# Layer 1 softmax: weighted values and sums of weights from one pass over the weights, the sums moved to their rows by a shuffle on VectorE

## The reference

```python
h = _rmsnorm(x, ln1_w)
qkv = jnp.einsum('bsh,oh->bso', h, wqkv)      # 16 q heads, 4 k and 4 v heads of 8
q, k = _apply_rope(q, cos, sin), _apply_rope(k, cos, sin)
scores = jnp.einsum('bqhd,bkhd->bhqk', q, k) * scale
scores = jnp.where(causal[None, None], scores, jnp.finfo(scores.dtype).min)
probs = jax.nn.softmax(scores, axis=-1)
attn = jnp.einsum('bhqk,bkhd->bqhd', probs, v).reshape(B, S, NH * HD)
x = x + jnp.einsum('bso,ho->bsh', attn, wo)
```

## Time and profile before

| | |
|---|---|
| median of 3 runs | 1948.61 us (1946.26 to 1956.49) |
| profiled execution, its own time | 1937.43 us |
| its span from first to last instruction | 1935.4 us |
| mean granted clock of TensorE | 0.960 |
| busy: PE / DVE / ACT / POOL | 1674.1 / 1238.5 / 1009.3 / 253.9 us |
| L1079, the two products | 3072 instructions, from 56.4 to 832.8 us |
| L1557, L1559, L2049 | 32 each |

### The profile page before, as it was taken

One profiled execution on the slowest core, in us unless ns is written; L12 is line 12 of the kernel. 1 busy time (PEld: TensorE's weight loads), 2 busy tenths in 40 slices (PEclk: granted clock), 3 DMA queues, 4 the chain that ended last, 5 costly groups with the idle time before them and its releaser, 6 DMA issues.

```text
span 1935.4 us, 65540 instructions
## 1 busy us (share of the span) xinstructions
PE 1674.1 (86%) x25348; PEld 1273.5 (66%) x25364; DVE 1238.5 (64%) x3535; ACT 1009.3 (52%) x2322; POOL 253.9 (13%) x271
## 2 busy tenths in 40 slices
PE   5999999979888898958998898897889889988866
PEld 3777776757666776745676676765577666676656
DVE  5677677756556666646676766765666666676535
ACT  3555555544555555524655566553544455544445
POOL 0000110000000000030111011101121112110063
PEclk9999999999999999979999999998999999999978
DMA  4333334431222211331222122210222111221244
GB/s 164 135 145 144 155 152 174 187 122 42 62 68 68 79 45 56 102 104 43 78 68 68 59 81 80 62 36 25 64 68 61 43 52 53 68 63 55 75 143 120
DMA packets 97379, 167.82 MB, mean 87 GB/s; under 512 B 15145, under 2 KB 65593, under 8 KB 93882
## 3 DMA queue, kind: packets, MB, share of 16 engines
q1 hardware_dynamic: 87322, 141.59, 21.8%
q0 software_dynamic: 9888, 23.71, 4.1%
HBM read 86.42 MB, written 78.80 MB: 85 GB/s over the span
## 4 chain that ended last, share of the span: by engine, by line
PE 52%; DVE 17%; issue 11%; ACT 11%; SPq 4%; DMA 2%; DVEq 1%; POOL 1%; POOLq 0%; ACTq 0%
PE psum L1007 5%; PE psum L851 4%; PE psum L885 3%; PE psum L997 3%; PE psum L1309 3%; PE psum L1199 3%; PE psum L1297 2%; PE psum L896 2%; PE psum L1045 2%; PE psum L932 2%; PE psum L1224 2%; PE psum L1093 2%; PE psum L936 2%; PE psum L1128 2%; ACT pts L1553 2%
## 5 line engine op out<-in xcount | busy, mean ns | idle before, releaser
L1553 ACT ACTIVATE pts<-psum 128x512 f32<-128x512 f32 x192 | 99.2, 604 | 162.1 <-PE psum L1045 161.4
L725 POOL DMA_INDIRECT rows<-h,recA x64 | 62.2, 972 | 780.7 <-DVE recA L1795 662.9
L1007 PE MATMUL psum<-wall,xT_s 128*128 128x512 f32 x256 | 130.3, 656 | 0.1
L749 POOL DMA_INDIRECT rows<-xn,recC x32 | 36.6, 1143 | 667.1 <-DVE recC L2249 612.9
L885 PE MATMUL psum<-txT,wall 128*128 128x128 f32 x864 | 117.0, 279 | 1.9 <-issue 1.5
L1158 PE MATMUL psum<-xT_s,wall 128*128 128x256 f32 x512 | 115.7, 379 | 0.0
L885 PEld LDWEIGHTS psum<-txT,wall 128*128 128x128 f32 x864 | 109.4, 197 | 4.5 <-issue 2.0
L896 PE MATMUL psum<-wall,tg 128*128 128x128 f32 (+1 forms) x720 | 109.2, 287 | 2.6 <-DVE tg L1743 1.9
L2058 DVE TENSOR_REDUCE mneg<-psum 128x2 f32<-128x512 f32 x128 | 79.4, 684 | 40.2 <-PE psum L1025 39.2
L1158 PEld LDWEIGHTS psum<-xT_s,wall 128*128 128x128 f32 x512 | 96.1, 190 | 13.2 <-issue 0.8
L896 PEld LDWEIGHTS psum<-wall,tg 128*128 128x128 f32 x720 | 94.8, 199 | 7.5 <-DVE tg L1743 5.2
(11 more groups left out here) (273 smaller groups left out, 4237.5 us busy)
## 6 DMA issues: line engine op xcount, KB each, us to landing
wall<-in_wB SPq DMA_DIRECT2D x84, 384.0 KB, 3.0
outs<-pbd SPq DMA_DIRECT2D x16, 1024.0 KB, 7.5
mixed_rows<-pbd SPq DMA_DIRECT2D x16, 899.5 KB, 9.6
wall<-in_wD SPq DMA_DIRECT2D x24, 578.0 KB, 3.7
tx<-rows SPq DMA_DIRECT2D x132, 64.0 KB, 2.8
rows<-pbd SPq DMA_DIRECT2D x64, 128.0 KB, 1.7
rows<-pbd SPq DMA_DIRECT2D x8, 1024.0 KB, 3.9
outs<-ty SPq DMA_DIRECT2D x108, 64.0 KB, 1.6
```

Source lines behind the costliest of these rows:

```text
L725: nc.gpsimd.indirect_dma_start(rows, bass.IndirectOffsetOnAxis(ap=slotsA[:, c:c + 1], axis=0), h2[:, t, :], None).then_inc(sem("scattered" ...
L1007: mm(bank(f"{name}{t}{c}"), xnT[:, t * P:(t + 1) * P], wqkv0[:, off + c * 512:off + (c + 1) * 512], start=True, stop=True).then_inc(*fills ...
L1553: af(pT[:, n, :], bank(f"e{n}"), ACT.Exp, scale=float(HD) ** -0.5).then_inc(*frees(f"e{n}"))
```

## The change

The sums of the weights are no longer made by matmuls of their own. The 32 columns of `v9` for one key head, of which 8 held values and 24 zeros, now hold 8 columns of values, 8 of zeros (by the parity of the query head) and, 16 columns on, 8 of ones and 8 of zeros in the same manner. Two of four query heads share one half of the bank's columns instead of all four sharing one, so one pass over `pT` gives a 128x256 result in which, of each 32 rows, the first 16 are values and the last 16 the sums that belong to them. `ones32` is gone.

On DVE a new step `sums_moved(t)` shuffles the bank into `rden` so that the sums stand on the rows of their values. ACT takes Ln and Exp of 128x256 there, and DVE's product is 128x256 and has two halves. `sums_moved(0)` stands where `weighted(0)` was, `weighted(0)` moves behind `rows_given`, and `sums_moved(1)` stands ahead of `weighted(1)`. The output projection adds two halves, with `woR` in two parts, so it has 4 matmuls a sequence instead of 2.

```diff
-        woR = wa[:, 5376:5504]
+        woR = wa[:, 5376:5632].rearrange("p (a n) -> p a n", a=2)
...
-        aT = aden[:, 0:N]
-        rden = aden[:, N:2 * N].rearrange("p (t n) -> p t n", t=NT)
+        aT = aden[:, 0:2 * N].rearrange("p (t a n) -> p t a n", t=NT, a=2)
+        rden = aden[:, 2 * N:4 * N].rearrange("p (t n) -> p t n", t=NT)
...
-            g.memset(ones32[:, :, :], 0.0).then_inc(sem("zeros"), 1)
-            g.wait_ge(sem("zeros"), 3)
+            g.wait_ge(sem("zeros"), 2)
             for j in range(GR):
-                r = j ^ 2
-                g.memset(ones32[:, j, r * HD:(r + 1) * HD], 1.0).then_inc(sem("zeros"), 1)
+                first = 2 * HD + j % 2 * HD
+                g.memset(v9[:, :, j, first:first + HD], 1.0).then_inc(sem("zeros"), 1)
...
                 for t in range(NT):
-                    last = mm(bank("wo")[:, t * P:(t + 1) * P], aT[:, t * P:(t + 1) * P], woR, start=True, stop=True)
+                    for a in range(2):
+                        last = mm(bank("wo")[:, t * P:(t + 1) * P], aT[:, t, a, :], woR[:, a, :], start=(a == 0), stop=(a == 1))
...
-                        for i in range(2):
-                            for j in range(GR):
-                                for g in range(NKV):
-                                    n = 4 * part + g
-                                    pe.wait_ge(*read_out(f"e{n}"))
-                                    values = v9[:, NKV * (part // 2) + g, j, :] if i == 0 else ones32[:, j, :]
-                                    last = mm(bank(f"pa{t}")[32 * g:32 * g + 32, i * P:(i + 1) * P], values, pT[:, n, j * P:(j + 1) * P],
-                                              start=(part == parts[0] and i == 0 and j == 0), stop=(part == parts[-1] and i == 1 and j == GR - 1))
+                        for j in range(GR):
+                            for g in range(NKV):
+                                n = 4 * part + g
+                                pe.wait_ge(*read_out(f"e{n}"))
+                                last = mm(bank(f"pa{t}")[32 * g:32 * g + 32, j // 2 * P:(j // 2 + 1) * P], v9[:, NKV * (part // 2) + g, j, :], pT[:, n, j * P:(j + 1) * P],
+                                          start=(part == parts[0] and j == 0), stop=(part == parts[-1] and j == GR - 1))
...
                 def inverse(t):
-                    act.wait_ge(*filled(f"pa{t}"))
-                    af(rden[:, t, :], bank(f"pa{t}")[:, P:2 * P], ACT.Ln).then_inc(*signals("act_chain"))
+                    act.wait_ge(*given("den_ready", t + 1))
+                    af(rden[:, t, :], rden[:, t, :], ACT.Ln).then_inc(*signals("act_chain"))
...
+                def sums_moved(t):
+
+                    dve.wait_ge(*filled(f"pa{t}"))
+                    dve.sem_inc(sem("copy_turn"), 1)
+                    v.stream_shuffle(rden[:, t, :], bank(f"pa{t}")[:, 0:2 * P], [16 + i % 16 for i in range(32)]).then_inc(*signals("den_ready"))
...
                 def weighted(t):
-                    dve.wait_ge(*filled(f"pa{t}"))
                     dve.wait_ge(*given("rden_ready", t + 1))
-                    v.tensor_tensor(aT[:, t * P:(t + 1) * P], bank(f"pa{t}")[:, 0:P], rden[:, t, :], ALU.mult).then_inc(*frees(f"pa{t}"))
+                    v.tensor_tensor(aT[:, t, :, :], bank(f"pa{t}")[:, 0:2 * P].rearrange("p (a n) -> p a n", a=2), rden[:, t, :].rearrange("p (a n) -> p a n", a=2), ALU.mult).then_inc(*frees(f"pa{t}"))
...
-                for first in (2 * HD, 2 * 32):
+                for first in (0, 2 * 32):
...
                 head_scale()
+                sums_moved(0)
+                rows_given()
                 weighted(0)
-                rows_given()
                 head_turned()
                 tile_step(6)
+                sums_moved(1)
                 weighted(1)
```

More of the change, by code:

```diff
@@ L183 @@
           "xnT_ready": 1, "xr_ready": 1, "x_free": 1},
-    "A": {"act_chain": 2, "kr_ready": 1, "kx_ready": 1, "dve_chain": 16, "ek": 4, "eq": 4, "k0_part": 3, "k0_ready": 1, "rden_ready": 2, "q0_part": 3, "q0_ready": 1, "rope_ready": 1, "aT_ready": 1, "o_ready": 2},
+    "A": {"act_chain": 2, "kr_ready": 1, "kx_ready": 1, "dve_chain": 16, "ek": 4, "eq": 4, "k0_part": 3, "k0_ready": 1, "den_ready": 2, "rden_ready": 2, "q0_part": 3, "q0_ready": 1, "rope_ready": 1, "aT_ready": 1, "o_ready": 2},
     "G": {"act_chain": 3, "counted": 1, "dve_chain": 14, "eg_ready": 1, "h2_free": 1, "h2_ready": 1, "lg_ready": 1, "recA_stored": 1, "rms2_rstd": 1, "x2_ready": 1, "scattered": 1, "slots_ready": 1},
@@ L267, in build @@
         v9 = v9s[:, 0:NT * NKV * GR * 32].rearrange("p (a j c) -> p a j c", a=NT * NKV, j=GR)
-        ones32 = sb("ones32", [P, GR, 32])
         pts = sb("pts", [P, 12 * 512])
-        aden = sb("aden", [P, 2 * N])
+        aden = sb("aden", [P, 4 * N])
         xk = x1
@@ L460, in build @@
         blk = ctx.enter_context(nc.Block())
-        NLOAD, NFIRST, ZEROS = [0], [0], 6 + GR
+        NLOAD, NFIRST, ZEROS = [0], [0], 5 + GR
         @blk.sync
@@ L2395 @@
     ang = np.concatenate([ang, ang], -1).T
-    woR = I["L0_ffn_wo"].T
+    woR = np.zeros((P, 2, D), np.float32)
+    for n in range(NHF):
+        g, j = n // GR, (n % GR) ^ 2
+        first = 32 * g + j % 2 * HD
+        woR[first:first + HD, j // 2] = I["L0_ffn_wo"].T[n * HD:(n + 1) * HD]
     ropec = np.zeros((P, 2, N), np.float32)
```

## The result

The kernel after takes 1962.97 us in the median (20 executions, 1957.32 to 1970.02), the kernel before 1950.62 on the same chip: ratio 1.0058, 95% interval 1.0048 to 1.0068. The forecast was 1962.3, in the range 1947 to 1977.

The account below looks back on a forecast made before the run. VectorE's chain at the body's end was taken to bound AHG, SyncE's queue to the load of x AHGBL. Terms 3.9 + 4.2 + 8.5 - 5.9 + 3.3 - 0.3 = +13.7 us on the median 1948.61 gave 1962.3, range 1947 to 1977.

Parts of the forecast that it names:

- AHG (3.9 + 7 x 0.52 + 8.5): AHG bodies: longer VectorE end +3.9 us, doubled output projection 0.52 us a body, clock falls +8.5 us.
- outside: Before the first slots and behind the last: longer load and memsets at the start counted 0; table has +0.5 us.
- the removed PE work returns nothing: Products for the sums, 2.7 us a body, 43 us in all, become idle time in AHG and AHGBL.
- The shuffle, the wider product, the doubled projection: AHG bodies: shuffle 0.34, load 0.08, product 0.34 for 0.20, together +0.56 us; projection +0.52 us.
- The clock in AHG: Idle of 2.7 us at AHG ends halves the clock at five of seven, 1.7 us each, +8.5 us.
- AHGBL: the failed step: AHGBL loop: slots +1.5 us, falls behind h mostly gone -8.9, longer moved falls +1.5; together -5.9 us.
- AGB: AGB body: start +1.5 us and a moved fall of about 2.4 us, end gains 0.5; +3.3 us net.
- R1: Not slower: AHG keeps its clock and AHGBL gets its own back; -1.5 us, 1947; chance 0.15.
- R2: Clock as it was everywhere: +10.3 us, 1959; chance 0.12.
- R3: Longer falls: every AHG end loses 3.1 us, AHGBL loses at both places; +36 us, 1984; chance 0.13.
- R4: Faster, PE is the bound after all: 16 x 1.6 = 26 us return, 1923; chance 0.05.
- R5: Shuffle costs its upper bound or drains DVE: +0.3 us at 7 + 7 places, +4 us, within the forecast's range.

Follow-up runs that it names:

- the pair again: Both kernels, before and after the change, profiled once more without an edit: spans 1947.0 us before and 1962.3 us after.
- before again: The kernel before, unchanged, profiled a second time: one execution, 1949.03 us, span 1947.0 us.
- after again: The kernel after, unchanged, measured and profiled a second time: 1959.25 us, ratio to before 1.0040.
- no shuffle: The kernel after without the two shuffles, ScalarE taking exponentials of the pass's result itself, output not normalised: 1953.58 us, ratio to before 1.0023.
- projection once: The kernel after with the output projection's products made once, half the heads left out of the output: 1959.93 us, ratio to before 1.0045.
- SyncE moved: The kernel after with 24 more semaphore instructions at the head of SyncE's program: 1959.21 us, ratio to before 1.0049.
- shuffle ahead: The kernel after with the first tile's shuffle ahead of head_scale and its product behind head_turned: 1953.16 us, ratio to before 1.0011.
- head early, one pass / two: Next group's head moved to the middle of the body: in the kernel after 1914.12 us, ratio 0.9814; in the kernel before 1938.64 us, 0.9935.
- pass twice: The kernel after with its one pass over the weights made twice into the same sums: 1964.22 us, ratio to before 1.0066.
- before: projection twice: The kernel before with each matmul of the output projection made twice, same result: 1956.6 us, ratio to before 1.0022.
- before: no sums: The kernel before without the matmuls that make the sums, ScalarE using the weights themselves, output not normalised: 1952.75 us, ratio 1.0001.

## Why the prediction was right in its total and wrong in its terms

Terms of the sum against both pairs of profiles, in us:

| | predicted | after less before | the pair again |
|---|---|---|---|
| AHG (3.9 + 7 x 0.52 + 8.5) | +16.0 | +10.2 | +10.4 |
| to AHGBL and in it | -5.9 | +9.8 | +9.8 |
| AGB and behind it (3.3 - 0.3) | +3.0 | +2.9 | -6.4 |
| outside | +0.5 | +8.3 | +1.5 |
| sum | +13.6 | +31.3 | +15.3 |

**That the removed PE work returns nothing: right.** No sums at all gives 1.0001 (0.9986 to 1.0016), where 26 to 43 us would have come back had PE been the bound.

**The shuffle, the wider product, the doubled projection: right in mechanism, a little too dear.** Where no fall is open the AHG period grew from 43.49 to 44.31, by 0.82; predicted were 1.08. Taking the shuffle away gives back 0.33, taking the doubling away 0.30, and by difference 0.19 is left for the wider product, Ln and Exp, which no run took apart. Load and shuffle are 0.45 us as rows, predicted 0.50. (The trace agrees with the Trainium skill, "VectorE: DVE Perf Modes", the perf-mode tier table, that no fast mode is to be hoped for: 0.44 us beside 0.41 for the copy of the same shape.) The round trip of shuffle, Ln and Exp in front of L2099 did stay hidden in AHG.

**The clock in AHG: mechanism right, size too large.** There are falls in AHG, where there had been none, and filling PE again removes them. But I expected five bodies to pay 1.7 us, 8.5 in all. Two paid, 3.0 and 1.6 us: 4.6. The step that failed is that the fall would come behind the second idle stretch of 2.7 us, on the next body's first projections. Five of six came behind the first, of about 1.6 us, and four of these slowed only a pass that had idle time behind it. That rows show no fall below 1.9 us of idle was also a misreading of the trace of before. In its second level half clock follows idle stretches of 1.22 and 1.47 us; the second of them, with the clock of the stretch behind it:

```profile
1592.65 1.22 PE L885 MATMUL psum<-txT,wall 128*128 128x128 f32 x8 [1.47 <-issue]
...
1593.62:1597.03 3.41, 3.41 (x66) 0.50 0.02 5
```

(That activity releases the clock, as the Trainium skill has it in "TensorE: Matmul & The Clock Gate", part 1, agrees with the falls that went when the pass was made twice.)

**AHGBL: the failed step, with the wrong sign, 15.7 us off.** I had the five falls behind h vanish and nothing else change. Timeline of PE in after, one body:

```profile
618.08 0.71 PE L894 MATMUL psum<-wall,tg 128*128 128x128 f32 x4 [2.44 <-DVE tg L1740]
620.45 0.69 PE L849 MATMUL psum<-ident,xr 128*128 128x128 f32 x2 [1.66 <-DVE aden L2051]
621.05 5.97 PE L1090 MATMUL psum<-xT_s,wall 128*128 128x256 f32 x16
...
638.75 0.43 PE L849 MATMUL psum<-ident,h 128*128 128x128 f32 x2 [3.17 <-DVE h L1990]
639.01 5.30 PE L1006 MATMUL psum<-wall,xT_s 128*128 128x512 f32 x8
```

and the granted clock in the stretches behind both idle times:

```profile
618.85:625.68 6.83, 5.23 (x13) 4.05 (x14) 2.08 (x5) 2.76 (x6) 2.41 (x3) 0.50 0.36 115
...
639.33:642.74 3.41, 3.41 (x5) 1.33 (x4) 3.41 (x7) 1.73 (x5) 0.00 (x0) 0.50 0.00 0
```

The idle before h did shrink, to 3.2 us (predicted 2.9), and the fall behind it from 6.8 us to 3.4, but it is there, which the prediction had named as a sign of being wrong, and the new one at the loop's start with it: from the first AHGBL slots to the last, 12 falls and 64.9 us at half clock against 7 and 44.4. What differs from the first profile of before, though, is on SyncE. Chain of waits of after from the record to the load of x, then that of before for the same instructions:

```profile
616.48 0.36 SPq L643
...
618.79 0.32 SPq L528
619.14 0.70 issue
619.90 0.70 issue
620.62 0.71 issue
621.37 0.70 SPq L530
622.07 0.69 issue
...
634.30 2.70 DMA x<-in_x
```

```profile
598.75 0.36 SPq L644
...
601.15 0.27 SPq L529
601.44 0.15 SPq L529
601.85 0.35 SPq L530
602.39 0.35 SPq L531
602.75 0.06 issue
```

At the first tile's load SyncE's instructions come 0.7 us apart in after. From the slots to the issue of the load of x, and from there to the next slots, it is:

| mean of five bodies, us | slots to load of x | load of x to next slots |
|---|---|---|
| before / before again | 16.05 / 17.06 | 44.03 / 43.04 |
| after / after again | 18.17 / 18.17 | 43.95 / 43.92 |
| no shuffle / projection once / SyncE moved | 17.57 / 17.65 / 17.67 | 43.85 / 43.62 / 43.69 |
| shuffle ahead | 17.40 | 43.36 |
| head early, one pass / two | 17.37 / 16.44 | 41.41 / 43.01 |
| pass twice / before: projection twice / before: no sums | 17.72 / 17.32 / 17.63 | 43.20 / 43.10 / 43.84 |

Against the first profile of before, whose chain runs through the load of x as that of after does, the whole 2.0 us a body are SyncE standing in a piece of its program that the change does not touch, and the stretch behind the load is the same (44.03 and 43.95) although the fall behind h is half as long: that gain of 8.9 us in all did not come. Against the second profile the sum can't be split so. There PE does not stand before the transpose of h. It stands 5.4 us at the loop's start, behind the late Ln, and half clock follows there and not behind h; that is the place to which the prediction had moved the falls of after, and the period is the same 60.1 us. What after loses against this typical execution is shown only as a sum, 2.0 us a body; that the load of x goes out 1.1 us later and that falls lie at both places are two parts of it, and no run took them apart. Why SyncE stands is open: it is not the one pass, since the kernel before with its projection doubled is at 17.32 us too, and moving SyncE's code by 24 instructions took off no more (0.5 us) than edits on other engines did. My prediction named this queue as the chain and then put no uncertainty on it.

**AGB: right for the profile shown, wrong for the typical execution.** The first profile of before was of its fastest execution, and as the other runs have it an untypically smooth one. In its second, and in all three two-pass or 128-instruction variants, AGB and the period behind it took 82.8 to 86.5 us; in every kernel with half the instructions in the pass they took 73.7 to 78.5. Here the one-pass kernel gains back 6.4 of the 9.8 us that it loses in AHGBL. That the shorter pass is what shortens this stretch the runs show; that PE's instructions reach it too late is an inference from the 0.7 us pieces, and no run made it separately.

**Rivals.** R1 was priced for an idle length between 1.9 and 2.3 us as the point that decides, and falls came behind 1.59 us; AHGBL did not get its clock back. R2 is refuted by the AHG falls, R3 happened in its second half only (falls at both places in AHGBL), R4 by the runs without sums. R5's upper bound for the shuffle, 0.7 us, was not reached. The total of the forecast was met by luck: measured less predicted, in the second pair, AHG is 5.6 us below, AGB 9.4 below, AHGBL 15.7 above and the rest 1.0 above, and these nearly cancel.

## What to carry to other kernels

Work taken from an engine that is not on the chain comes back only after the chain has been moved onto it: here the same edit cost 7 to 12 us with the next group's head at the end of the body and saved 24.5 us with it in the middle. Before a filler is removed, look at what will be idle around it and what runs first after the idle time: a fall of the clock costs nothing if it lands on work with slack behind it. And profile the kernel before twice when single-digit microseconds matter: the first profile of before, 0.7% under the median, lacked a stall in AGB that its second profile and three variants had (AGB 58.0 to 59.5 us against 52.3).

## What the runs showed of the hardware

- An engine can start its instructions 0.7 us apart although the trace shows nothing that they wait for: PE in the unrolled AGB body behind 112 instructions of a pass (100 in the kernel with the pass made twice), SyncE in the AHGBL loop. The kernel before showed it on PE in one execution (AGB 59.51 us) and not in the other (52.26). The cause is open.
- In five of six AHGBL bodies of the second profile of before ScalarE's Ln started 5.1 us after the end of PE's pass that it waits for, and in the first profile 0.1 us after it, with the same period of 60.1 us: PE's idle time only changed places, from before h (4.94 us) to the loop's start (5.4 us).
- The pattern load of the shuffle (LOAD_MASK_SELECT) takes 0.01 us, and the shuffle starts in the same hundredth of a microsecond.
- TensorE's clock fell to half behind an idle stretch of 1.59 us following a busy body in after, and behind 1.47 us in before, when 1.93 us elsewhere in before had brought no fall. A fall of 3.41 us with idle time behind it cost nothing (period 44.31 us); one of 10.24 us that reached the next body's first projections cost 3.0.
